# A transformer block with two expert layers around an attention: tokens routed in two sides, results stored in tile order and gathered by token on GpSimd, first attention pair inside the second expert pass

## The chip, the cores and the metric

The kernel runs on one core of one Trainium2 chip. The time is the device time of one execution, in microseconds (us), as the median of some runs. A profiled execution gives the rows shown below; their times count from the start of its span.

## The reference

4096 tokens of 128 channels (16 sequences of 256) pass an expert layer (FFN), an attention, and the same expert layer again. Each part adds to the residual:

```python
x = x + 0.5 * ffn(layernorm(x), Wg, bg, Wgu, bgu, Wd, bd)
x = x + attention(layernorm(x), W_attn, b_attn, W_proj, b_proj)   # 16 heads of 8 channels, causal
x = x + 0.5 * ffn(layernorm(x), Wg, bg, Wgu, bgu, Wd, bd)

def ffn(xt):                                # 16 experts, the best 2 of each token
    top_vals, top_idx = jax.lax.top_k(xt @ Wg.T + bg, 2)
    rw = softmax(top_vals)
    # of each chosen expert e: gate and up are the even and odd columns of xt @ Wgu[e] + bgu[e]
    gated = (clip(up, -7, 7) + 1.0) * (min(gate, 7) * sigmoid(1.702 * min(gate, 7)))
    out_e = gated @ Wd[e] + bd[e]           # the two are summed, weighted with rw
```

## The kernel before, in words

All engines run streams of their own, written by hand, with semaphores between them. Tokens lie in 32 tiles of 128; four tiles are a quad (`q`, 8 of them). `f` is 0 for the first expert layer and 1 for the second.

**Router.** Per quad, VectorE normalises the rows, TensorE transposes them and makes the logits, VectorE takes the best two and the rank of each token in its expert. GpSimd (POOL) then scatters the rows with indirect DMAs of 128 rows each into `rows_by_expert` in DRAM, 8 per quad, 64 in all. A row has 129 numbers: the last one is the number under which its result is to be stored (`K_NUM`); ScalarE copies each row for the second expert (`copy_rows`). In the second layer, the router of quads 0 to 5 (`MERGED`) runs inside the last turn of the attention.

**Table.** When all ranks are there, VectorE works out which expert and which rows each of 80 tiles has: 64 full ones' worth of rows, and 16 that pad each expert to a multiple of 128. SyncE (SP) copies the ends of the experts into `tab`, SP and ScalarE (ACT) zero 8 tiles each behind the last rows (`zero_tiles`), and SP copies the table into `tab`. `s_tab` counts these copies, and ScalarE and VectorE wait for it.

**Expert pass.** 80 tiles, two at a time (a pair `k`, four pairs a turn `t`, 40 pairs): SP loads the rows into `xt`, waiting for `s_goes` and `s_xTp` of the pair four before; TensorE transposes them (L1487), multiplies with gate and up (L1500) and down (L1512); ScalarE copies the weights (L717), evacuates the transposes and takes the sigmoid; VectorE gates (L1097 to L1100) and adds the down bias into `ysb` (L1128). It also makes the store targets (`going` L1106, `goes_to` L1124). GpSimd scatters each result tile by token number into `results_by_token` (L582), two per pair. `expert_pipeline` shifts the steps: in slot n, TensorE transposes pair n-1, does gate and up of pair n-2 and down of pair n-4.

**Attention.** When all results are stored, GpSimd loads them by quads with one plain DMA (`yg`); VectorE adds them weighted to `x_resident` (`combine`, L749), makes the statistics and normalises. TensorE transposes and projects q, k and v (L1155, L1161, L1168). q and k are split into three bf16 parts, which SP writes to DRAM several times over and reads back as `q_stack` and `k_stack`. The first scores need both stacks. Of 8 quads, quad x+2 is combined while quad x is in attention.

**Tail.** After the second expert pass the results are read with eight plain DMAs of SP and ScalarE, combined (L1140) and written out by quads.

## Time and the profile before

| | us |
|---|---|
| median of 3 runs | 784.53 (783.05 to 786.78) |
| the profiled execution's own time | 784.48 |
| its span | 782.8 |
| first scatters end, first expert pass begins (gate and up) | 103.7, 113.4 |
| first scores of the attention | 258.7 |
| second pass begins (gate and up) | 644.7 |
| last store issued, last combine ends | 752.9, 780.1 |

The span is what the engines' records cover; the time of the execution is 1.7 us longer. The stretches between the lines are: router, expert pass, first pair, attention with the second router, expert pass, tail.

### The profile page before, as it was taken

The page shows a single profiled execution, that of the slowest core. Times are in us where ns is not written, and L with a number is a line of the kernel's source. Part 1 is how long each engine was busy: PE and PEld are TensorE (multiplying, and loading weights), DVE is VectorE, ACT ScalarE, POOL GpSimd, SP SyncE. Part 2 cuts the span into 40 slices and gives each one's busy share as a digit, 9 for nine tenths or more (in the row PEclk, how much of TensorE's full clock was granted, in tenths as well). Part 3 has the DMA queues.
Part 4 walks back from the last instruction along what each step waited for, and adds up shares of the span by engine and source line. Part 5 has one row for each costly group of instructions (what it writes and reads, how often), then busy time and mean ns, then how long its engine had stood idle before and what let it go on. Part 6 is the DMA issues. An engine that isn't in the chain of part 4 may idle for free.

```text
span 782.8 us, 19236 instructions
## 1 busy us (share of the span) xinstructions
PE 514.2 (66%) x5867; PEld 328.6 (42%) x5867; DVE 512.6 (65%) x2750; ACT 300.9 (38%) x554; POOL 334.5 (43%) x348
## 2 busy tenths in 40 slices
PE   3368429888504579787978897978775319888600
PEld 2234117656302245454544454545452207655400
DVE  6865408777624577777777777879874507877618
ACT  1111028766201245353544454625342217766300
POOL 2777745777740010101010101020657744777740
PEclk9999999999855689897989798989896559999955
DMA  9411363333215170606060606050111163333237
GB/s 270 142 55 51 79 89 99 107 105 104 68 55 202 62 242 7 239 29 215 0 242 22 224 2 216 15 202 2 42 43 53 58 104 87 110 107 102 79 121 234
DMA packets 83468, 83.88 MB, mean 107 GB/s; under 512 B 10373, under 2 KB 74314, under 8 KB 83146
## 3 DMA queue, kind: packets, MB, share of 16 engines
q1 hardware_dynamic: 68618, 56.78, 24.4%
q0 software_dynamic: 10368, 23.15, 8.8%
q10 hardware_dynamic: 4416, 3.16, 1.8%
q8 instruction: 31, 0.51, 0.3%
q14 instruction: 35, 0.29, 0.1%
HBM read 43.03 MB, written 39.99 MB: 106 GB/s over the span
## 4 chain that ended last, share of the span: by engine, by line
DVE 23%; POOL 23%; PE 23%; issue 22%; DMA 4%; ACT 3%; DVEq 2%; SPq 1%; POOLq 0%; ACTq 0%
POOL results_by_token L582 12%; POOL rows_by_expert L549 10%; DVE by_token L799 5%; PE banks L1293 2%; DVE x_resident L1140 2%; PE banks L1243 2%; PE banks L1269 2%; DVE x_resident L749 2%; PE banks L1420 2%; PE banks L1218 2%; PE banks L1168 1%; PE banks L1161 1%; PE banks L1271 1%; PE banks L1234 1%; DVE upc L1098 1%
## 5 line engine op out<-in xcount | busy, mean ns | idle before, releaser
L582 POOL DMA_INDIRECT results_by_token<-ysb,goes_to x160 | 154.1, 963 | 73.8 <-issue 44.8
L799 DVE CUSTOM_DVE_ANT_0 by_token<-banks,konst_sb 128x128 f32<-128x128 f32 (+1 forms) x512 | 147.1, 352 | 38.3 <-issue 38.1
L616 ACT ACTIVATE pT<-banks 128x1536 f32<-128x1536 f32 x64 | 92.8, 1450 | 53.4 <-PE banks L1271 53.4
L717 ACT ACTIVATE pT<-w_experts 128x384 f32 x160 | 74.9, 516 | 69.7 <-DMA tab<-tabc 42.8
L1500 PE MATMUL banks<-xT,pT 128*64 128x128 f32 x1280 | 90.0, 284 | 10.4 <-DVE row_buf L1100 9.0
L549 POOL DMA_INDIRECT rows_by_expert<-by_token,posi x80 | 77.0, 963 | 28.5 <-issue 23.2
L1500 PEld LDWEIGHTS banks<-xT,pT 128*64 128x64 f32 x1280 | 70.7, 140 | 27.5 <-DVE row_buf L1100 16.5
L517 POOL CAST q_parts<-sig 128x512 bf16<-128x512 f32 x7 | 4.2, 604 | 152.4 <-DVE sig L787 152.4
L1487 PE MATMUL banks<-konst_sb,xt 128*128 128x128 f32 x160 | 35.6, 306 | 46.6 <-DMA xt<-rows_by_expert 45.9
L1512 PE MATMUL banks<-pT,row_buf 128*64 128x128 f32 x640 | 52.9, 285 | 15.5 <-DVE ysb L1128 13.1
L610 ACT ACTIVATE mT<-banks 128x256 bf16<-128x256 f32 x64 | 24.6, 384 | 92.3 <-PE banks L1218 92.3
L1293 PE MATMUL banks<-pT,by_token 128*32 128x256 f32 (+1 forms) x1024 | 59.6, 354 | 0.0
L1199 PE MATMUL banks<-k_stack,q_stack 64*128 64x256 bf16 x256 | 42.4, 288 | 22.1 <-DVE mraw L799 13.5
L1512 PEld LDWEIGHTS banks<-pT,row_buf 128*64 128x64 f32 x640 | 37.1, 139 | 27.7 <-issue 24.5
L1128 DVE TENSOR_TENSOR ysb<-banks,w_experts 128x128 f32<-128x128 f32 x160 | 39.2, 286 | 11.6 <-issue 0.2
L1243 PE MATMUL banks<-q_stack,k_stack 64*128 64x256 bf16 x256 | 44.5, 294 | 0.0
L1234 PE MATMUL banks<-mT,select 64*128 64x256 bf16 x256 | 44.0, 296 | 0.0
L729 ACT ACTIVATE sig<-banks 128x256 f32<-128x256 f32 x80 | 30.7, 384 | 34.3 <-PE banks L1500 28.9
L1293 PEld LDWEIGHTS banks<-pT,by_token 128*32 128x32 f32 x1024 | 28.1, 116 | 34.8 <-issue 25.0
L1218 PE MATMUL banks<-identb,mparts 128*64 128x128 bf16 x256 | 20.7, 245 | 33.6 <-DVE x_resident L820 20.3
L1097 DVE SCALAR_TENSOR_TENSOR sig<-banks,sig 128x256 f32<-128x256 f32 x80 | 33.8, 423 | 13.4 <-ACT sig L729 11.1
L1487 PEld LDWEIGHTS banks<-konst_sb,xt 128*128 128x128 f32 x160 | 16.6, 145 | 61.7 <-issue 58.1
(182 smaller groups left out, 1123.5 us busy)
## 6 DMA issues: line engine op xcount, KB each, us to landing
xt<-rows_by_expert SPq DMA_DIRECT2D x160, 64.5 KB
q_stack<-q_by_part SPq DMA_DIRECT2D x8, 1024.0 KB, 6.4
k_stack<-k_by_part SPq DMA_DIRECT2D x8, 1024.0 KB, 5.8
q_by_part<-q_parts SPq DMA_DIRECT2D x16, 384.0 KB, 3.1
k_by_part<-k_parts SPq DMA_DIRECT2D x16, 384.0 KB, 2.8
yg<-results_by_token POOLq DMA_DIRECT2D x8, 512.0 KB, 4.9
results_by_token<-ysb,goes_to POOLq DMA_INDIRECT x160
x_resident<-in_x SPq DMA_DIRECT2D x8, 256.0 KB, 5.5
```

Of the source, the lines that this page charges most:

```text
L549: pool.indirect_dma_start(out=rows_dram, out_offset=bass.IndirectOffsetOnAxis(ap=posi[:, c:c + 1], axis=0), in_=rows_of(f, q)[:, i, k, :], ...
L582: pool.indirect_dma_start(out=results_dram, out_offset=bass.IndirectOffsetOnAxis(ap=goes_to[:, 2 * k + i:2 * k + i + 1], axis=0), in_=ysb[ ...
L616: nc.scalar.activation(pT[:, s % 2, :], banks[:, 3:6, :].rearrange("p a q -> p (a q)"), ACT.Exp, scale=SCALE).then_inc(a_exp, 1)
L717: last = nc.scalar.activation(w_tile[:, 2 * k + i, :], w_all[:, bass.ds(experts[key][k % 2 * 2 + i], EW)], ACT.Identity)
L799: last = nc.vector.tensor_tensor_reduce(masked[:, (3 * g + qt) * P:(3 * g + 2 * qt + 1) * P], of, lag, 1.0, NEG * NEG_BELOW, ALU.add, ALU. ...
L1199: return nc.tensor.matmul(bank[1 + g % 2][:, c:c + T], q[r, pair, m, o + P:o + T], k[r, pair, m, o:o + T], start=g // 2 == 0, stop=g // 2 ...
L1234: nc.tensor.matmul(bank[3 + g % 2][:, g // 2 * T:(g // 2 + 1) * T], select[maxima(g), g, :], mT[maxima(g), s % 2, :], start=g // 2 == 0, s ...
L1243: nc.tensor.matmul(bank[3 + g % 2][:, c:c + T], k[r, pair, m, o:o + P], q[r, pair, m, o:o + T], start=False, stop=False)
L1293: last = nc.tensor.matmul(bank[6][g * QUARTER:(g + 1) * QUARTER, c + kt * P:c + T], of_head, w, start=j == 0 and kt == 0, stop=j == GRP - ...
L1487: last = nc.tensor.transpose(bank[k % 2][:, i * P:(i + 1) * P], xt[:, 2 * k + i, 0:C], ident)
L1500: last = nc.tensor.matmul(bank[2 + k % 2][h * HALF:(h + 1) * HALF, at:at + P], w_tile[:, 2 * k + i, which * F + h * HALF:which * F + (h + ...
L1512: last = nc.tensor.matmul(bank[6 + k % 2][h * HALF:(h + 1) * HALF, i * C:(i + 1) * C], gT[:, k, i * P + h * HALF:i * P + (h + 1) * HALF], ...
```

## The change

The tokens are routed in two sides of 16 tiles each, with counts, ranks and a table of their own. Each side has 32 tiles of rows and again 16 of padding, so 48 tiles (24 pairs, 6 turns) per pass, and there are now four passes `p` (0 and 1 in the first layer, 2 and 3 in the second), with 96 tiles per layer instead of 80. `expert_passes` runs the two passes of a layer without draining the pipeline in between.

```diff
-REGION = N + P
-TILES = N * TOPK // P + E
+SIDES = 2
+REGION = N // SIDES + P
+TILES = TSIDE * TOPK + E
```

SP does all zero tiles (16 a side) and, new, the stores of the results in tile order; it waits for them in its own order:

```diff
         def zero_tiles(eng, g):
-            with eng.Fori(0, E // 8) as e:
+            with eng.Fori(0, E // 4) as e:
...
+            def store(p, t, k):
+
+                sp.wait_ge(s_ysb[k], p * TURNS + (t + 1))
+                sp.dma_start(results_t[p % SIDES][:, bass.ds(t * DUOS + k, 1), :, :], ysb[:, k:k + 1, :, :]).then_inc(s_store[k], 16)
...
+                table_of(first)
+                sp.wait_ge(s_zero, 16 * (1 + E * (first + 1)))
+                sp.wait_ge(s_scat[0], 16 * TOPK * TSIDE * (f + 1))
+                load_turn(first, 0)
+                table_of(second)
+                experts(first)
+                sp.wait_ge(s_zero, 16 * (1 + E * (second + 1)))
+                sp.wait_ge(s_scat[1], 16 * TOPK * TSIDE * (f + 1))
+                load_turn(second, 0)
+                experts(second)
+                for k in range(1, DUOS):
+                    store(second, TURNS - 2, k)
+                for k in range(DUOS):
+                    if f == 0 and k == 1:
+                        stack_first(sp)
+                    store(second, TURNS - 1, k)
```

ScalarE and VectorE wait for both tables of a layer before its first pass:

```diff
+                def copy_weights(p, t, k):
+                    if p % SIDES == 0 and isinstance(t, int) and (t, k) == (0, 0):
+                        act.wait_ge(s_tab, 32 * (p + 2))
```

Rows have 128 numbers again, `copy_rows`, `going` and `goes_to` are gone. VectorE works out where each token's two results lie (`in_tiles`, 3 instructions a side), and GpSimd gathers them with one indirect DMA per 128 rows, 8 per quad: into `yg` for the attention, into `by_token` for the tail, side by side.

```diff
+            def gather(q, to, done):
+                for j in range(QUAD * TOPK):
+                    c = q * QUAD * TOPK + j
+                    pool.indirect_dma_start(
+                        out=to[:, j, :], out_offset=None,
+                        in_=results_dram[q // QSIDE], in_offset=bass.IndirectOffsetOnAxis(ap=tilepos[:, c:c + 1], axis=0)).then_inc(done, 16)
...
+                    for q in range(NQ):
+                        if q % QSIDE == 0:
+                            stored(SIDES + q // QSIDE)
+                        gather(q, last_results[:, q * QUAD * TOPK:(q + 1) * QUAD * TOPK, :], s_got[q])
```

The first attention pair is prepared by hooks in the last two turns of pass 1; on VectorE:

```diff
+                if (t, k) == (TURNS - 2, 0):
+                    combine(0)
+                if (t, k) == (TURNS - 2, 1):
+                    stats(0)
+                if (t, k) == (TURNS - 2, 2):
+                    normalise(0)
+                if (t, k) == (TURNS - 1, 1):
+                    parts_of_first(0)
+                if (t, k) == (TURNS - 1, 2):
+                    parts_of_first(1)
+                if (t, k) == (TURNS - 1, 3):
+                    combine(1)
+                if (t, k) == (TURNS, 0):
+                    stats(1)
+                if (t, k) == (TURNS, 1):
+                    normalise(1)
```

How the instructions stand now is shown at three places. On SP, in the loop of an expert pass, two pairs of one turn stood so before (L471 loads a tile of rows, L1592 reads row numbers from the table, ISA is address arithmetic):

```order
L1592 TENSOR_LOAD tab
L471 ISA
L471 DMA xt<-rows_by_expert 128x129
L471 ISA
L471 DMA xt<-rows_by_expert 128x129
L479 REGISTER_ALU
```

and one pair of the same loop stands so now (L459 loads, L464 stores two tiles at once):

```order
L459 ISA [waits s_xTp]
L459 DMA xt<-rows_by_expert 128x128
L459 ISA
L459 DMA xt<-rows_by_expert 128x128
L463 REGISTER_ALU
L464 ISA [waits s_ysb1]
L464 DMA results_by_tile<-ysb 128x2x128
```

Each pair has a third DMA on SP and a wait for VectorE's `ysb` between the loads of two pairs.

On SP, between the first loads of pass 2 and the loads behind them, the second table of the layer stands now (the loop L409 runs four times, four zero tiles each):

```order
L442 DMA tab<-zrow 1x16x1 [waits s_ends]
L409 UNCONDITIONAL_BRANCH [waits s_tab_ends]
L1644 TENSOR_LOAD tab
L411 DMA rows_by_expert<-zeros 128x128
L409 COMPARE_AND_BRANCH
L451 DMA tab<-tabc 1x48x1 [waits s_table]
L1644 TENSOR_LOAD tab [waits s_tab]
L459 ISA [waits s_xTp]
```

Before, there was one table of a layer, ahead of all loads, and its loop ran twice on SP and twice on ScalarE.

On VectorE, slot 16 of pass 1 (the gate of a pair, its `ysb`, then the hook) reads now:

```order
L1140 SCALAR_TENSOR_TENSOR sig<-banks,sig 128x256 [waits s_sig]
L1141 TENSOR_SCALAR upc<-banks 128x256
L1143 SCALAR_TENSOR_TENSOR gT<-upc,sig 128x256 [waits s_vec]
L1157 ISA [waits s_y,s_store0]
L1157 TENSOR_TENSOR ysb<-banks,w_experts 128x128
L755 SCALAR_TENSOR_TENSOR x_resident<-yg,wts,x_resident 128x128 [waits a_got]
L755 SCALAR_TENSOR_TENSOR x_resident<-yg,wts,x_resident 128x128 x3
```

The L755 instructions stood behind the whole pass before and now stand between two gates.

## Rows read from the trace of the kernel before

**Rows 1.** The page, chain that ended last: its costliest lines, share of the span.

```profile
POOL results_by_token L582 12%; POOL rows_by_expert L549 10%; DVE by_token L799 5%; PE banks L1293 2%; DVE x_resident L1140 2%; PE banks L1243 2%; PE banks L1269 2%; DVE x_resident L749 2%; PE banks L1420 2%; PE banks L1218 2%; PE banks L1168 1%; PE banks L1161 1%; PE banks L1271 1%; PE banks L1234 1%; DVE upc L1098 1%
```

**Rows 2.** The chain into the first pass: start us, length us, what.

```profile
103.70 4.93 DMA rows_by_expert<-by_token,posi
...
110.17 0.04 SPq L471
...
110.68 0.04 SPq L471
...
110.82 1.90 DMA xt<-rows_by_expert
```

**Rows 3.** GpSimd timeline, scatters: start us, us, what, idle before and its releaser.

```profile
64.57 0.96 POOL L549 DMA_INDIRECT rows_by_expert<-by_token,posi  x1 [0.31 <-issue]
65.83 0.95 POOL L549 DMA_INDIRECT rows_by_expert<-by_token,posi  x1 [0.30 <-issue]
```

**Rows 4.** TensorE timeline, first pass: its start, and down of two pairs.

```profile
113.44 1.98 PE L1500 MATMUL banks<-xT,pT 128*64 128x128 f32 x16
...
120.29 0.61 PE L1512 MATMUL banks<-pT,row_buf 128*64 128x128 f32 x8
...
122.12 0.61 PE L1512 MATMUL banks<-pT,row_buf 128*64 128x128 f32 x8
```

**Rows 5.** Two stretches: length, then PE, PEld, DVE, ACT, POOL busy, clock, DMA, GB/s.

```profile
229.00:253.00 24.00, 8.46 (x29) 4.10 (x29) 13.26 (x52) 2.57 (x4) 3.65 (x4) 0.50 0.43 145
440.00:480.00 40.00, 34.53 (x464) 20.03 (x456) 31.36 (x193) 20.19 (x26) 5.35 (x6) 0.91 0.42 137
```

**Rows 6.** VectorE timeline, one pair of the first pass and the next one's gate.

```profile
121.35 0.41 DVE L1097 SCALAR_TENSOR_TENSOR sig<-banks,sig 128x256 f32<-128x256 f32 x1
...
122.53 0.15 DVE L1124 COPY goes_to<-going 128x2 int32<-128x2 int32 x1
122.83 0.49 DVE L1128 TENSOR_TENSOR ysb<-banks,w_experts 128x128 f32<-128x128 f32 x2
...
123.30 0.42 DVE L1097 SCALAR_TENSOR_TENSOR sig<-banks,sig 128x256 f32<-128x256 f32 x1
```

**Rows 7.** SP timeline, first table: last four zero tiles, table copies.

```profile
97.08 1.88 SPq L414 DMA_DIRECT2D rows_by_expert<-zeros  x4
99.17 1.20 SPq L458 DMA_DIRECT2D tab<-tabc  x2
```

**Rows 8.** SP timeline, second table: the experts' ends, eight zero tiles.

```profile
622.08 0.59 SPq L446 DMA_DIRECT2D tab<-zrow  x1
624.45 5.05 SPq L414 DMA_DIRECT2D rows_by_expert<-zeros  x8
```

**Rows 9.** DMA issues, 88 to 111 us: count, KB each, median us to landing.

```profile
tab<-tabc SPq DMA_DIRECT2D x2, 0.3 KB, 7.6
```

**Rows 10.** VectorE timeline, first and last instruction of the first table.

```profile
90.93 0.21 DVE L1060 TENSOR_SCALAR zrow<-banks,konst_sb 16x1 int32<-16x1 f32 x1 [0.37 <-PE banks L1474]
...
93.83 0.17 DVE L1084 CAST tabc<-tabf 128x2 int32<-128x2 f32 x1
```

**Rows 11.** Timeline of all engines, last copy of the k parts, first scores.

```profile
247.01 0.46 SPq L400 DMA_DIRECT2D k_by_part<-k_parts  x1
...
258.68 0.39 PE L1199 MATMUL banks<-k_stack,q_stack 64*128 64x256 bf16 x1 [5.32 <-DMA k_stack<-k_by_part]
```

**Rows 12.** Timeline of all engines, the second pass begins.

```profile
639.05 0.94 ACT L717 ACTIVATE pT<-w_experts 128x384 f32 x2 [18.35 <-DMA tab<-tabc]
640.37 4.70 SPq L471 DMA_DIRECT2D xt<-rows_by_expert  x8
...
644.70 1.98 PE L1500 MATMUL banks<-xT,pT 128*64 128x128 f32 x16
```

**Rows 13.** The chain in the tail: start us, length us, what.

```profile
754.18 2.22 DMA results_by_token<-ysb,goes_to
...
776.69 2.20 DVE x_resident L1140 x8
```

More of the change, by code:

```diff
@@ new lines, in load_turn, with experts, stores_behind @@
+            def load_turn(p, t):
+                for k in range(DUOS):
+                    if k % 2 == 0:
+                        rows = registers(nc, sp, tab[0:1, p % SIDES, bass.ds(t * UNROLL + (TILES + 2 * k), 4)], SIDES * E * REGION)
+                    load(p, t, k, rows)
+                    stores_behind(p, t, k)
+            def experts(p):
+                load_turn(p, 1)
+                with sp.Fori(2, TURNS) as t:
+                    load_turn(p, t)
+            def stores_behind(p, t, k):
+                back = 2 if k < DUOS - 1 else 1
+                if not isinstance(t, int) or t >= back:
+                    store(p, t - back, (k + 1) % DUOS)
+                elif p % SIDES:
+                    store(p - 1, t - back + TURNS, (k + 1) % DUOS)
@@ L1132, in _, with later @@
+                def later(p, t, k):
+                    if (p, t) == (2, 0):
+                        if k == 0:
+                            in_tiles(2)
+                        if k == 2:
+                            in_tiles(3)
+                expert_passes(dve, f, (2, gate), (4, evac_y), chain=(ch, 2), hook=first_pair if f == 0 else later)
                 if f == 0:
@@ L1611, in slot, with turn @@
             turn, k2 = t + pair // DUOS, pair % DUOS
[L1612 removed]
+            if isinstance(turn, int) and turn >= TURNS:
                 continue
[L1614 to L1629 removed]
+            if isinstance(turn, int) and turn < 0:
+                if p % SIDES:
+                    step(p - 1, turn + TURNS, k2)
+                continue
+            step(p, turn, k2)
+        if hook and isinstance(t, int):
+            hook(p, t, k)
+    def turn(p, t):
+        for k in range(DUOS):
+            slot(p, t, k)
+    for p in range(f * SIDES, (f + 1) * SIDES):
+        peeled = 2 if p == 1 else 0
+        turn(p, 0)
+        turn(p, 1)
+        with eng.Fori(2, TURNS - peeled) as t:
+            if chain:
+                chain[0].begin(t - 2, chain[1] * DUOS)
+            turn(p, t)
+        if chain:
+            chain[0].end(TURNS - peeled - 2)
+        for t in range(TURNS - peeled, TURNS):
+            turn(p, t)
+    for k in range(DUOS):
+        slot(f * SIDES + 1, TURNS, k)
 _OUT = (B, T, C)
```

684 lines of the change are left out of this document (330 added, 354 removed).

## The prediction

> **What bounds the kernel now.** I read the page's chain first. Its two costliest lines are GpSimd's: the scatter of results, 12% of the span, and the scatter of rows, 10% [rows 1]. One scatter starts 1.26 us after the one before it (0.96 of work, 0.30 between) [rows 3]. A result tile costs one such scatter, so a pair of tiles costs 2.52 us, whatever the other engines do. Next comes what these could do. In the stretch before the four result buffers are full, TensorE issues down for two successive pairs 1.83 us apart [rows 4], and VectorE needs 1.95 us per pair, of which 0.30 is the copy of the targets and 0.07 what `going` adds [rows 6]: without both, about 1.58. So 40 pairs at 2.52 are GpSimd's time, and the pass is slower than its engines.
>
> Three stretches between passes are waits: the first pass starts only when all 64 row scatters have landed (the last one at 103.7 plus 4.9, then the loads; gate and up at 113.4) [rows 2, 4]; from the last result to the first scores at 258.7 one pair is prepared on a nearly idle core (TensorE 8.5 and VectorE 13.3 us busy in 24) [rows 5, 11]; the tail is one load and a chain of combines [rows 13].
>
> **Part by part.** I go through the kernel on the clock of the trace of before, and take two things for granted: the attention itself and the second router keep their length, and there I shift the clock.
>
> *First pass, start.* It needs only the 32 scatters of side 0, long done by then, but ScalarE's weight copies wait for both tables. VectorE's router is lengthened by the table of side 0, 3.1 us (90.9 to 94.0 [rows 10]), while GpSimd has a backlog of scatters and nobody else waits. So side 1's ends come at about 94.1. From there SP: 2.4 us to the first zero tile [rows 8]; then 16 tiles instead of 8. Four take 1.88 [rows 7]; two rounds take 5.05 [rows 8], so 1.29 lie between rounds, and four rounds are 11.4. Then 0.2 and two table copies in 1.2 [rows 7]. Their landing was 7.6 us from issue behind 16 zero tiles from two queues [rows 9]; one queue asks for half as much per us, and a small copy that finds the queues free lies within the 2.4 above [rows 8]. I take 3 from issue (bounds 2 and 7.6). Together 17.6 us, so both tables are there at 111.8 (110.8 to 116.4), weights 0.94 later plus 0.4 [rows 12], gate and up at 113.2. That is the start of before: nothing gained, the wait for scatters is replaced by one for SP.
>
> *Rate.* GpSimd is out of the loop, but SP gets a third DMA per pair. Two issues start 0.51 us apart [rows 2]. A turn of four pairs is now 12 of them, 6.1; the round's own cost (a register load and branch, 1.29 less the ordinary gap) about 0.9; a second register load 0.4; arithmetic and waits 0.3; and a store of 256 rows issues perhaps in 0.37 to 0.46 instead of 0.33 (the nearest is the copy of k parts, 0.46 [rows 11]), 0.3 per turn. That is 8.0 us per turn, **2.0 us per pair**: slower than TensorE's 1.83. Bounds: 1.83, if SP's instructions overlap or come cheaper, and 2.3, if every DMA of the turn takes the 0.46 (12 times 0.13 more). SP has four pairs of lead, so only its rate counts. Load 8 goes at about 119.4, load 47 at 39 × 2.0 later, 197.4; it is issued in 0.9 and lands in 1.9 [rows 2]: slot 48 at 200.2. Of the stores' traffic I count nothing: the 16 DMA engines are 43% busy at most in the stretches shown [rows 5].
>
> *First pair in pass 1.* VectorE's 13.3 us [rows 5], all but the last normalise (1.1), now lie in slots 40 to 48: 12.2, less 9 × 0.42 that it has free per slot, less some 2 that it may lag behind: 6.4. TensorE's part (8.5 at clock 0.50, so 4.2 at full) is covered by that. `ysb` of pair 44 is then ready at 209.1, and SP turns to the stacks: spreading q and k is six issues (2.8, at 0.46 each), and from the start of the last one to the scores it was 11.7 [rows 11], about 14.0 in all. **First scores at 223.1 instead of 258.7: 35.6 us saved.** Gather 1 starts behind the root of pair 0 (about 190.5) and lands at 203, when VectorE reaches it; if it is late, that comes on top. In the attention eight gathers per quad are 10.1 us of GpSimd in about 43 us, where it was busy 5.35 in 40 [rows 5]: they fit between the parts of one pair and the next.
>
> *Second pass, start.* Ends of side 0 at 622.1 [rows 8], its table at +17.6, 639.7; then eight loads (0.4 and 4.7 [rows 12]) to 644.8; and only then SP does side 1's table: another 17.6, 662.4. ScalarE waits for it, gate and up at 663.7 instead of 644.7 [rows 12]. **19.0 us lost.** What was hidden behind the scatters before is now in the open, twice, on one queue. The second `in_tiles` delays one gate in the filling pipeline, some 1 us, inside my rounding.
>
> *To the end.* Load 8 at 669.9 (half clock at the start), load 47 at 747.9, slot 48 at 750.7, last `ysb` 7.8 us later (four slots) at 758.5, stored by 761.2 (issue 0.5, landing 2.2 as the scatter's [rows 13]). Side 0's 32 gathers start when its stores have landed, near 717, and end near 758, just free. Side 1's begin at 761.2 and are all exposed: 32 × 1.26 = 40.4, 801.6, landing 1.3 after the last one's end. The trace has no gather; the nearest is the scatter of the same 128 rows of 512 bytes, so 1.26 it is (a gather at 0.96 back to back would save 9.6; with 0.3 more it costs 9.6). The last quad's combine (2.3) and the way out (2.7: before, from 780.1 to 782.8) give 807.9. The tail from the last result was 28.6 us (754.2 to 782.8) and is 49.4 now.
>
> **Sum.** 807.9 − 35.6 = 772.3, plus the 1.7 by which the profiled execution (784.48) exceeds its span: **774 us**. That execution is within 0.1 of the median of the runs shown, so I compare with 784.5: 10.5 faster, 1.3%.
>
> **A page against it.** Of SP the trace shows 0.51 us per issue, and that rate paces my passes. The Trainium skill ("DMA: Bandwidth & Descriptors", Issuing engines are not separate DMA queues) holds that starting DMAs on several engines saves only the time to initiate them, usually small beside the DMA itself. By the rows a load's issue is a fourth of its landing, and three a pair exceed TensorE's 1.83; by the page's view the move to SP would be nearly free, which is the first rival.
>
> **Rivals.**
> 1. *TensorE paces the passes.* For it: 1.83 was held for several pairs, and my 2.0 is built from parts, not seen. Against: the parts are all SP's own instructions, one behind the other. 39 × 0.17 twice is 13.3 less: 761. Chance 0.18.
> 2. *SP paces them still slower.* One mechanism: the store's 256 rows hold the queue, so that it and the loads behind it issue in 0.46 rather than 0.33. The trace has both: zero tiles in a row kept their pace, the copies of parts in a row did not. From 2.0 + 10.5/78 = 2.14 us per pair on the gain is gone; at 2.3 it is 78 × 0.3 = 23 more: 797, slower than before. About 0.17 for the part beyond 2.14, with 2.2 (790) its middle.
> 3. *GpSimd and VectorE block each other in the tail.* Combines now run beside gathers, both of them at SBUF. Before, scatters kept their 0.96 while VectorE worked on the router beside them [rows 3], which speaks against it; but no row has them beside combines. If each combine (2.2 per quad) stopped the gathers, side 1's four cost 9: 783, no change. Chance 0.08. The Trainium skill ("SBUF — State Buffer", Who interferes with whom) describes such a lock for VectorE operations with two SBUF inputs against a GpSimd operation that reads SBUF; no row here shows it.
> 4. *The tables come earlier or later than I think*, with landings at the ends of their bounds: 3 × 1 less, or 3 × 4.6 more (788). Chance 0.07, mostly no change.
>
> My forecast has 0.50 (766 to 780 by itself, from landings and VectorE's lag of ±2 each and a rate of ±0.05).
>
> **Numbers.** The range reaches to rival 1 below and to the middle of rival 2 above: 757 to 790. Below 757 and above 790 I leave 0.08 and 0.12. A measurement of this kernel tells 0.5%, some 4 us, from no change. Faster (below 780.6): my case nearly whole, rival 1, a little of the others, 0.69. Same: the edge of my case, rivals 3 and 4, 0.14. Slower: rival 2 and late tables, 0.17.
>
> **What the changed profile would show.** SP's loads 2.0 us apart per pair in the middle of a pass, with TensorE's transposes waiting for `xt`, and no gap between passes; gate and up of pass 0 at 113, of pass 2 some 40 us behind the last ends' copy (it was 22.6); first scores at 223; side 1's gathers back to back 1.26 apart for 40 us with TensorE silent. I am wrong if the loop on SP is not the pace, if the first gather is late for VectorE, or if the gathers in the attention push the parts of a pair behind its scores.

## The result: slower, where faster was forecast

| | before | after |
|---|---|---|
| median, us | 786.16 (783.05 to 787.12, 5 runs) | 791.99 (790.80 to 795.07, 5 runs) |
| ratio | | 1.0087, 95% interval [1.0055, 1.0119] |
| span of the profiled execution, us | 782.8 | 793.3 |

The change costs 0.9%. The forecast was 774 us; 792 lies outside its range, on the other side of no change.

How the stretches came out, on the clock of each profiled execution (the forecast's own points, and those of the rows below):

| stretch | before | forecast | after | after − forecast |
|---|---|---|---|---|
| to gate and up of the first pass | 113.4 | 113.2 | 110.7 | −2.5 |
| from there to the first scores | 145.2 | 109.9 | 128.4 | **+18.5** |
| to the copy of side 0's ends, second layer | 363.4 | 363.4 | 363.1 | −0.3 |
| to gate and up of the second pass | 22.6 | 41.6 | 38.3 | −3.3 |
| to the first exposed gather | | 97.5 | 104.8 | **+7.3** |
| to the end of the span | | 46.7 | 47.9 | +1.2 |

The last column adds up to 20.9, and 772.3 + 20.9 is the span, within rounding. The attention kept its length, and the two losses that were forecast (a later second pass, a tail of gathers) came in at nearly their size. What failed is the gain at the first pair, and the pace of the passes in both layers.

### The profile page after: what moved, and what is told of

Its sections match the earlier page's. It is cut to its first block, busy times and chain, and to the rows that moved or that the text cites. A ratio compares the mean times of both kernels' runs of the same rounds, so it can differ in the third digit from the quotient of the medians.

```text
span 793.3 us, 19957 instructions
## 1 busy us (share of the span) xinstructions
PE 531.3 (67%) x6287; PEld 353.9 (45%) x6287; DVE 525.7 (66%) x2691; ACT 317.9 (40%) x602; POOL 296.9 (37%) x308
## 4 chain that ended last, share of the span: by engine, by line
PE 29%; DVE 21%; SPq 18%; issue 16%; POOL 7%; DMA 3%; ACT 3%; DVEq 1%; ACTq 0%; POOLq 0%
SPq L459 8%; DVE by_token L805 5%; SPq L464 4%; POOL by_token L526 4%; POOL rows_by_expert L564 3%; PE banks L1469 3%; SPq L411 2%; PE banks L1327 2%; PE banks L1553 2%; PE banks L1517 2%; SPq L1644 2%; PE banks L1277 2%; PE banks L1303 2%; DVE x_resident L755 2%; PE banks L1461 2%
## 5 line engine op out<-in xcount | busy, mean ns | idle before, releaser
L564 POOL DMA_INDIRECT rows_by_expert<-by_token,posi x120 | 115.7, 964 | 57.2 <-issue 35.0
L1553 PE MATMUL banks<-xT,pT 128*64 128x128 f32 x1536 | 109.3, 286 | 31.3 <-ACT pT L731 17.0
L731 ACT ACTIVATE pT<-w_experts 128x384 f32 x192 | 90.0, 516 | 77.4 <-DMA tab<-tabc 61.7
L1553 PEld LDWEIGHTS banks<-xT,pT 128*64 128x64 f32 x1536 | 85.6, 141 | 48.5 <-ACT pT L731 31.8
L526 POOL DMA_INDIRECT by_token<-results_by_tile,tilepos x64 | 61.4, 959 | 105.5 <-DMA results_by_tile<-ysb 86.6
L526 POOL DMA_INDIRECT yg<-results_by_tile,tilepos x64 | 61.6, 963 | 81.1 <-DMA results_by_tile<-ysb 62.7
L1140 DVE SCALAR_TENSOR_TENSOR sig<-banks,sig 128x256 f32<-128x256 f32 x96 | 40.6, 423 | 62.2 <-ACT sig L741 60.7
L1564 PE MATMUL banks<-pT,gT 128*64 128x128 f32 x768 | 59.5, 276 | 4.4 <-DVE ysb L1157 4.4
L1157 DVE TENSOR_TENSOR ysb<-banks,w_experts 128x128 f32<-128x128 f32 x192 | 46.7, 283 | 15.6 <-issue 12.7
L1564 PEld LDWEIGHTS banks<-pT,gT 128*64 128x64 f32 x768 | 45.9, 139 | 5.4 <-DVE gT L1143 5.1
L1461 PE MATMUL banks<-konst_sb,by_token 128*128 128x128 f32 x60 | 14.4, 384 | 46.3 <-DVE by_token L932 38.3
L1541 PEld LDWEIGHTS banks<-konst_sb,xt 128*128 128x128 f32 x192 | 20.4, 146 | 54.5 <-issue 43.6
```

Of the source, the lines that this page charges most:

```text
L526: pool.indirect_dma_start(out=to[:, j, :], out_offset=None, in_=results_dram[q // QSIDE], in_offset=bass.IndirectOffsetOnAxis(ap=tilepos[: ...
L564: pool.indirect_dma_start(out=rows_dram, out_offset=bass.IndirectOffsetOnAxis(ap=posi[:, c:c + 1], axis=0), in_=rows_of(f, q)[:, i, :], in ...
L731: last = nc.scalar.activation(w_tile[:, 2 * k + i, :], w_all[:, bass.ds(held[key][k % 2 * 2 + i], EW)], ACT.Identity)
L1157: last = nc.vector.tensor_tensor(ysb[:, k, i, :], bank[6 + k % 2][:, i * C:(i + 1) * C], w_all[:, bass.ds(held[key][k % 2 * 2 + i] + EW, C ...
L1541: last = nc.tensor.transpose(bank[k % 2][:, i * P:(i + 1) * P], xt[:, 2 * k + i, :], ident)
L1553: last = nc.tensor.matmul(bank[2 + k % 2][h * HALF:(h + 1) * HALF, at:at + P], w_tile[:, 2 * k + i, which * F + h * HALF:which * F + (h + ...
```

## The profile after

The page's chain, by engine and by line, share of the span:

```profile
PE 29%; DVE 21%; SPq 18%; issue 16%; POOL 7%; DMA 3%; ACT 3%; DVEq 1%; ACTq 0%; POOLq 0%
SPq L459 8%; DVE by_token L805 5%; SPq L464 4%; POOL by_token L526 4%; POOL rows_by_expert L564 3%; PE banks L1469 3%; SPq L411 2%; PE banks L1327 2%; PE banks L1553 2%; PE banks L1517 2%; SPq L1644 2%; PE banks L1277 2%; PE banks L1303 2%; DVE x_resident L755 2%; PE banks L1461 2%
```

Where GpSimd's scatters stood [rows 1], SP's queue stands now: loads L459, stores L464, zero tiles L411, table loads L1644. The scatter of results is gone, the 32 exposed gathers are L526.

SP's timeline in the middle of pass 0 (start us, length us, what):

```profile
138.06 0.85 SPq L459 DMA_DIRECT2D xt<-rows_by_expert  x2
139.20 0.41 SPq L464 DMA_DIRECT2D results_by_tile<-ysb  x1
...
146.25 0.85 SPq L459 DMA_DIRECT2D xt<-rows_by_expert  x2
```

Two loads and a store per pair, and the next turn begins 8.19 us after this one: 2.05 us per pair, where I had worked out 2.0. But the loop has rows of another kind in it. The same timeline 20 us later, and the DMA queues of that moment (queue, packets, MB, share of the 16 engines):

```profile
157.43 2.17 SPq L459 DMA_DIRECT2D xt<-rows_by_expert  x2
```

```profile
q1 hardware_dynamic: 571, 0.27, 34.6%
q8 instruction: 1, 0.02, 3.4%
```

Two loads take 2.17 us instead of 0.85, and a 16 KB block of instructions is fetched in just these 3 us (157.6 to 159.2 by its packet). Over the whole trace 12 of SP's 288 loads and stores take more than 0.6 us, 10.9 us in excess of the ordinary 0.34, and 10 of the 12 lie over such a fetch. In all, load 47 of pass 1 goes 82.7 us behind load 8 (2.12 per pair), and the forecast had 78.0.

SP's timeline at the start of pass 0, and its longest wait there:

```profile
109.14 7.69 SPq L459 DMA_DIRECT2D xt<-rows_by_expert  x8
119.80 0.41 SPq L464 DMA_DIRECT2D results_by_tile<-ysb  x1
120.97 0.86 SPq L459 DMA_DIRECT2D xt<-rows_by_expert  x2
```

```profile
SPq L464 <- DVE ysb L1157: 3.0, 1, 3.0
```

Load 8 stands behind the store of pair 0 on SP, and SP waits 3.0 us for that pair's `ysb`. So load 8 goes 10.3 us behind the first gate and up, where the forecast had 6.2; in pass 2 it goes 9.7 behind.

VectorE's timeline over three hooks (L755 combine, L773 statistics, L785 normalise; the gate is L1140):

```profile
192.40 2.31 DVE L755 SCALAR_TENSOR_TENSOR x_resident<-yg,wts,x_resident 128x128 f32<-128x128 f32 x8
194.62 0.41 DVE L1140 SCALAR_TENSOR_TENSOR sig<-banks,sig 128x256 f32<-128x256 f32 x1
...
199.32 1.11 DVE L785 TENSOR_SCALAR xnT<-x_resident,a_mv,a_rs 128x128 f32<-128x128 f32 x4
200.34 0.41 DVE L1140 SCALAR_TENSOR_TENSOR sig<-banks,sig 128x256 f32<-128x256 f32 x1
...
203.20 0.42 DVE L1140 SCALAR_TENSOR_TENSOR sig<-banks,sig 128x256 f32<-128x256 f32 x1 [1.25 <-ACT sig L741]
...
207.27 0.42 DVE L1140 SCALAR_TENSOR_TENSOR sig<-banks,sig 128x256 f32<-128x256 f32 x1 [2.16 <-ACT sig L741]
```

and TensorE's in the same slots:

```profile
200.57 0.63 PE L1189 MATMUL banks<-konst_sb,xnT 128*128 128x128 f32 x4 [2.15 <-DVE xnT L785]
...
220.03 0.66 PE L1564 MATMUL banks<-pT,gT 128*64 128x128 f32 x8 [2.86 <-DVE ysb L1157]
223.98 1.09 PE L1189 MATMUL banks<-konst_sb,xnT 128*128 128x128 f32 x4 [3.29 <-DVE xnT L785]
```

Gates come 2.8 to 4.1 us apart. First VectorE is full and TensorE waits for it, for 5.4 us of it in hooks of its own (the transposes of L1189 need `xnT`). Then it is the other way round: VectorE is idle 1.25 and 2.16 for a sigmoid whose matmuls are late. Part of that is the granted clock, which fell from 1.00 to 0.50 for 3.4 us at 202.0. Two stretches of 2 us show it (columns as in [rows 5]), first of this kernel and then of a second execution of it on another chip, `e2_control` below:

```profile
202.00:204.00 2.00, 2.00 (x18) 1.67 (x14) 0.77 (x3) 0.77 (x3) 1.48 (x2) 0.50 0.65 175
202.00:204.00 2.00, 2.00 (x24) 1.41 (x24) 1.37 (x5) 1.70 (x4) 1.53 (x2) 1.00 0.75 203
```

In that stretch 16 matmuls of gate and up take 1.40 us and not 1.09, and the two of L1195 2.05 and not 1.13; gate and up of pair 43 comes 4.4 us behind that of pair 42, in the control 2.7.

SP's timeline behind the hooks, and the first scores:

```profile
220.33 1.02 SPq L389 DMA_DIRECT2D q_by_part<-q_parts  x2
...
223.92 0.96 SPq L394 DMA_DIRECT2D k_by_part<-k_parts  x1
225.27 0.70 SPq L397 DMA_DIRECT2D q_stack<-q_by_part  x1
230.09 0.37 SPq L397 DMA_DIRECT2D k_stack<-k_by_part  x1
```

```profile
239.08 0.39 PE L1233 MATMUL banks<-k_stack,q_stack 64*128 64x256 bf16 x1 [12.96 <-DMA k_stack<-k_by_part]
```

From the start of the last copy into `k_by_part` (the spreading of the parts) to the scores it is 15.2 us, where it was 11.7 [rows 11].

The second layer's tables on SP, and the pass behind them:

```profile
602.19 0.57 SPq L442 DMA_DIRECT2D tab<-zrow  x1
604.95 11.06 SPq L411 DMA_DIRECT2D rows_by_expert<-zeros  x16
616.23 1.18 SPq L451 DMA_DIRECT2D tab<-tabc  x2
619.23 4.33 SPq L459 DMA_DIRECT2D xt<-rows_by_expert  x8
623.62 0.52 SPq L442 DMA_DIRECT2D tab<-zrow  x1
625.93 10.31 SPq L411 DMA_DIRECT2D rows_by_expert<-zeros  x16
636.45 1.16 SPq L451 DMA_DIRECT2D tab<-tabc  x2
```

```profile
640.53 1.76 PE L1553 MATMUL banks<-xT,pT 128*64 128x128 f32 x14 [17.02 <-ACT pT L731]
```

This is the serial chain of the forecast, step by step: 16 zero tiles in 11.06 and 10.31 (forecast 11.4), twice, with TensorE idle. In the tail GpSimd's gathers run back to back, 1.25 us apart, beside VectorE's combines:

```profile
745.36 0.94 POOL L526 DMA_INDIRECT by_token<-results_by_tile,tilepos  x1 [3.25 <-DMA results_by_tile<-ysb]
746.61 0.94 POOL L526 DMA_INDIRECT by_token<-results_by_tile,tilepos  x1 [0.30 <-issue]
...
784.16 0.95 POOL L526 DMA_INDIRECT by_token<-results_by_tile,tilepos  x1 [0.30 <-issue]
786.70 2.32 DVE L1177 SCALAR_TENSOR_TENSOR x_resident<-by_token,wts,x_resident 128x128 f32<-128x128 f32 x8 [7.66 <-DMA by_token<-results_by_tile,tilepos]
```

## The experiments

The runs were made on several chips. On two of them (the runs e1 and e3) the kernel before took 927 us instead of some 785, so these runs are compared only with each other, stretch by stretch (none of them is the changed kernel unedited); the runs e2 and e4 are on chips that take 788 and 783 us for it.

### On the chip that takes 927 us

**One store for two pairs**, `e1_store_two` (SP: 10 DMAs per turn instead of 12; VectorE and GpSimd wait for the stores that are left):

```diff
             def store(p, t, k):
-
-                sp.wait_ge(s_ysb[k], p * TURNS + (t + 1))
-                sp.dma_start(results_t[p % SIDES][:, bass.ds(t * DUOS + k, 1), :, :], ysb[:, k:k + 1, :, :]).then_inc(s_store[k], 16)
+                if k % 2 == 0:
+                    return
+                sp.wait_ge(s_ysb[k], p * TURNS + (t + 1))
+                sp.dma_start(results_t[p % SIDES][:, bass.ds(t * DUOS + k - 1, 2), :, :], ysb[:, k - 1:k + 1, :, :]).then_inc(s_store[k], 16)
```

> The changed kernel with one edit: SP stores two pairs (four tiles) with one DMA instead of one pair, so a turn of an expert pass has 10 DMAs on SP and not 12. Theory A (SP's DMA issues pace the passes at 2.05 us per pair): two issues of 0.51 us less per turn give 1.8 us per pair, where TensorE's 1.83 takes over; some 78 pairs x 0.2 = 16 us less, about 776 us against 792. Rival B (the pace is set elsewhere, by transfers or by the long issues of 1 to 2 us that come every 10 us or so in SP's loop): less than 4 us, about 790.

**Zero tiles on two engines**, `e1_split_zero`:

```diff
-        def zero_tiles(eng, g):
-            with eng.Fori(0, E // 4) as e:
+        def zero_tiles(eng, g, half):
+            with eng.Fori(0, E // 8) as e:
...
+                for p in (2 * f, 2 * f + 1):
+                    act.wait_ge(s_tab_ends, 16 * (p + 1))
+                    zero_tiles(act, p % SIDES, 1)
```

> The changed kernel with one edit: of each side's 16 zero tiles ScalarE issues 8 and SP 8, two rounds of four on each, as before the change there were for a layer. Theory A (SP's serial tables are the wait ahead of both layers' passes): two rounds are 5.05 us and four were 11.4, so each table is 6.3 us shorter; pass 2 has two in the open, pass 0 one: gate and up of pass 2 at 628 and not 640.5, of pass 0 at 105 and not 110.7, 19 us less in all, 773. Rival B (zero tiles from two queues make the table's copies land later, 7.6 us as in the kernel before and not 3): half of that is given back, 783.

**The first pair behind the pass**, `e1_late_pair`:

```diff
         if hook and isinstance(t, int):
-            hook(p, t, k)
+            if p != 1:
+                hook(p, t, k)
...
-        peeled = 2 if p == 1 else 0
+        peeled = 0
...
+    if hook and f == 0:
+        for t in range(TURNS - 2, TURNS + 1):
+            for k in range(DUOS):
+                hook(1, t, k)
```

> The changed kernel with the first attention pair prepared behind pass 1 instead of in its last two turns (the hooks of all engines are called after the last slot, SP starts the stacks behind all stores). Theory A (the hooks made slots 40 to 48 of pass 1 some 10 us longer, so they hid only part of their work): first scores at 246 and not 239.1, 7 us more, 799. Rival B (all of the 15 us of VectorE's and TensorE's work was hidden): 15 us more or beyond, 807.

**A tail of plain loads**, `e1_plain_tail`:

```diff
-                        gather(q, last_results[:, q * QUAD * TOPK:(q + 1) * QUAD * TOPK, :], s_got[q])
+                        at = q % QSIDE * QUAD * TOPK * P
+                        pool.dma_start(last_results[:, q * QUAD * TOPK:(q + 1) * QUAD * TOPK, :],
+                                       results_dram[q // QSIDE][at:at + QUAD * TOPK * P, :].rearrange("(n p) c -> p n c", p=P)).then_inc(s_got[q], 16)
```

> The changed kernel, but in the tail GpSimd loads each quad's 1024 result rows with one plain DMA in tile order instead of eight gathers by token (the order by token is left out, so the results are combined with the wrong tokens). Theory A (side 1's 32 gathers, 38.8 us back to back behind the last store, are all exposed): the tail from the last store's landing falls from 48.8 to about 22 us, 27 us less, 765. Rival B (the loads of 512 bytes per row and the combines bound the tail as well): 15 us less, 777.

Measured, where the kernel before took 926.8: 935.8 (store_two), 945.3 (split_zero), 946.9 (late_pair), 884.2 (plain_tail). Four readings hold within this chip:

- *Zero tiles.* In the second layer it is 39.1 us from the start of VectorE's first table to gate and up with the tiles split, and 48.4 in late_pair, whose tables are the unedited ones. SP's timeline of split_zero, second table:

```profile
733.39 0.52 SPq L442 DMA_DIRECT2D tab<-zrow  x1
735.75 4.94 SPq L411 DMA_DIRECT2D rows_by_expert<-zeros  x8
740.91 1.16 SPq L451 DMA_DIRECT2D tab<-tabc  x2
743.73 1.93 SPq L459 DMA_DIRECT2D xt<-rows_by_expert  x4
```

  4.94 against 10.31, and the copies land no later (2.8 us from issue to the next load either way): theory A for the zero tiles, 9.3 of the 12.6 us that it gives for pass 2, and rival B's late copies are not there. Theory A's gain ahead of pass 0 did not come: gate and up is at 134.2 there, and at 131.1 to 131.7 in the other three, because VectorE made side 1's ends 6.7 us later (115.5 for 108.8 in late_pair).
- *The tail.* From the last down matmul to the end it is 21.5 us with plain loads and 51.9 and 51.8 in split_zero and late_pair; in the changed kernel on its first chip it was 51.8. So the gathers cost 30 us there, theory A.
- *The first pair* came to its scores no later than with the hooks (136 us behind the first gate and up, 139 and 141 in split_zero and plain_tail). Neither theory allowed for that.
- *The stores* brought the scores 10 us nearer to the first gate and up (130).

### The same edits beside the changed kernel

> The changed kernel itself, once more: the chip of the last four runs took 927 us for the kernel before, where 786 had been measured, so differences there say little against runs elsewhere. Both theories: the ratio to the kernel before is 1.009 on a chip that takes 785 us for it; if this chip too is slow, all comparisons of this call are made with this run.

> One store on SP for two pairs, as in e1_store_two, now beside a run of the changed kernel. Theory A (SP's issues pace the passes): 16 us less than the changed kernel, of which 8 are there at the first scores. Rival B (pace set elsewhere): less than 4 us.

> The first attention pair prepared behind pass 1, as in e1_late_pair, now beside a run of the changed kernel. Theory A (the hooks hide part of their work): first scores some 7 us later than in the changed kernel, counted from the first gate and up. Rival B (all of the 15 us were hidden): 15 us later. Rival C (the hooks cost the pass as much as they hide; on the slow chip the scores came no later than without them): within 3 us.

**The tables rearranged**, `e2_tables`:

```diff
                     if isinstance(t, int) and (t, k) == (0, 0):
-                        act.wait_ge(s_tab, 32 * (p + 2))
+                        act.wait_ge(s_tab[p % SIDES], 32 * (f + 1))
...
-                table_of(first)
+                table_of(sp, first)
...
                 load_turn(first, 0)
-                table_of(second)
                 experts(first)
...
                     for q in range(MERGED - 1, NQ):
                         scatter(q)
+                    table_of(pool, 3)
...
                     positions(MERGED - 1)
+                    table(2)
```

(the same on VectorE, and `table_of(pool, 1)` behind the scatters of the first layer.)

> The changed kernel with the tables rearranged: GpSimd copies the ends, zeroes the tiles and copies the table of side 1 behind its last scatter of each layer, SP does side 0's alone; ScalarE and VectorE wait only for the table of the pass that they begin; VectorE makes side 0's table of the second layer in the middle of the router of the last two quads and not behind it. Theory A (the gaps ahead of passes 0 and 2 are SP's serial tables and nothing else): gate and up of pass 0 at 98 and not 110.7, of pass 2 some 5 us behind VectorE's last table instead of 22, at 606 and not 640.5; 46 us less in all, ratio to the kernel before 0.95. Rival B (what is behind them is also late: the row scatters of side 1, or GpSimd's 19 DMAs at 1 us each beside the pass): half of it is given back, ratio 0.98.

| | median us | ratio to before, interval | gate/up 0 | first scores | VectorE's ends of side 0 | gate/up 2 | last down | end |
|---|---|---|---|---|---|---|---|---|
| e2_control | 791.9 | 1.0043 [1.0025, 1.0062] | 110.4 | 237.9 | 601.4 | 640.0 | 740.3 | 792.3 |
| e2_store_two | 770.1 | 0.9757 [0.9722, 0.9792] | 110.6 | 227.4 | 589.3 | 627.6 | 718.7 | 770.9 |
| e2_late_pair | 793.1 | 1.0074 [1.0049, 1.0100] | 110.4 | 238.3 | 596.5 | 635.0 | 734.1 | 786.0 |
| e2_tables | 744.9 | 0.9452 [0.9410, 0.9495] | 97.7 | 222.8 | 567.3 | 590.2 | 690.2 | 744.4 |

*Stores.* 22 us, more than theory A's 16: 10.7 from gate and up to the first scores, 9.2 in passes 2 and 3. The same 70 us of passes 0 and 1 in both kernels (length, then PE, PEld, DVE, ACT, POOL busy with their instructions, clock, DMA share, GB/s), the changed kernel first:

```profile
120.00:190.00 70.00, 63.71 (x902) 51.46 (x902) 55.71 (x174) 55.31 (x139) 7.60 (x8) 1.00 0.47 132
```

```profile
120.00:190.00 70.00, 67.89 (x970) 55.26 (x966) 60.17 (x198) 59.11 (x149) 7.61 (x8) 1.00 0.53 144
```

A pair is 26 matmuls, so 902 are 34.7 pairs, 2.02 us each, and 970 are 37.3, 1.88 each. In the waits of the first window TensorE stands 6.2 us for `xt` (12 times, 1.9 the longest); in the second it is 0.7 us, once, and SP has fallen from 18% of the chain to 6%:

```profile
PE 43%; DVE 22%; issue 13%; POOL 9%; SPq 6%; ACT 3%; DMA 3%; DVEq 1%; ACTq 0%; POOLq 0%
```

In store_two 9 issues are still long, 8 of them over a 16 KB fetch, for 8.6 us in excess, and in this window TensorE hardly waits for a load. The pace itself gives what theory A said: gate and up comes 6.9 us earlier at pair 40, ahead of the first hook, and 9.1 at the last pair of passes 2 and 3 (0.19 per pair), 16.0 together. The rest of the gain is a side effect of the edit. Without a store of its own, pair 44 no longer stands ahead of the stacks, so SP begins the spreading 0.5 us behind `ysb` of pair 43 (99.8 us behind gate and up, and 107.2 in the control), 4.0 before `ysb` of pair 44 is there; and from the spreading to the scores it is 17.0 and not 20.4. The hooked slots give 4.0 of the 6.9 back; the clock fell in them (6.8 us at 0.50).

*The pair behind the pass.* Rival C: 127.8 us from gate and up to the first scores, and 127.5 with the hooks. SP's timeline without them:

```profile
222.78 0.90 SPq L389 DMA_DIRECT2D q_by_part<-q_parts  x2
...
226.26 1.19 SPq L394 DMA_DIRECT2D k_by_part<-k_parts  x1
...
232.57 0.37 SPq L397 DMA_DIRECT2D k_stack<-k_by_part  x1
```

In the control the spreading starts at 217.54, 5.2 us earlier, but the scores come 20.4 us behind it and not 15.5. The pass itself is 14.0 us longer with the hooks (last down at 222.9 and not 208.9, from the same start). At `ysb` of pair 44, behind which SP turns to the stacks, it is 10.3 us later (106.7 and 96.4 behind gate and up), and some 0.7 of that was there before the first hook. Neither of the two executions has the fall of the clock in these slots. (The profiled execution of late_pair ended 5 us below its median; that lies behind the first scores, where it took 358 us to the ends of side 0 and the others 362 to 364.) The DMA queues from the first spreading to the scores (queue, packets, MB, share of the 16 engines), in the control and then in late_pair:

```profile
q1 hardware_dynamic: 4645, 4.71, 72.3%
q0 software_dynamic: 256, 0.52, 12.1%
```

```profile
q1 hardware_dynamic: 3584, 4.19, 84.4%
q0 software_dynamic: 160, 0.33, 9.8%
```

The DMA engines are over 0.8 busy in this stretch. With the hooks the last stores of the pass and a whole gather are in it (eight DMAs; late_pair has five such there), 5.23 MB in 20.4 us for 4.52 in 15.5. At the rate of late_pair (0.29 MB per us) the 0.71 MB more are 2.4 of the 4.9 us. But the bytes alone don't set the length: store_two moves 5.42 MB in this stretch of its own, in 17.0 us. What goes with the length is when GpSimd's gather for the third pair starts. It starts 2.3 us behind the first spreading in the two profiles of the changed kernel, in e2_tables and in three of the runs on the chips that take 927 us, and there the stretch takes 18.1 to 20.4. It starts 6.7 to 9.5 behind it in the other runs with hooks, and there the stretch takes 15.9 to 17.9. In late_pair one gather is over 2 us behind the first spreading and the next begins 11.3 behind it, with 15.5. No run moved that gather alone.

*Tables.* Theory A, 47 us: pass 0 begins at 97.7, behind the router and no longer behind SP, and pass 2 at 590.2, 4.5 us behind the start of VectorE's last table (585.65):

```profile
97.65 1.76 PE L1555 MATMUL banks<-xT,pT 128*64 128x128 f32 x14
```

```profile
569.81 10.39 SPq L411 DMA_DIRECT2D rows_by_expert<-zeros  x16
...
583.97 9.88 SPq L458 DMA_DIRECT2D xt<-rows_by_expert  x14
```

Side 0's zero tiles lie beside the router now. (Its ends come 19 us earlier here because VectorE makes that table earlier, so that column does not compare.) Of the 47.9 us of span, 12.7 lie ahead of pass 0, 2.4 up to the first scores, 34.7 from there to gate and up of pass 2; the tail is 2.1 longer. The three parts of the edit were not run one by one. Side 1's row scatters run until 603 us, beside pass 2, and cost nothing that the span shows: the pass takes 100.0 us from gate and up to the last down, the control's 100.3.

### Together

> The changed kernel with two edits together, the rearranged tables (alone 745 us where the changed kernel took 792) and one store for two pairs (alone 770). Theory A (the waits for the tables and SP's pace are separate, each in its own stretch): the gains add, 47 + 22 = 69 us, 723. Rival B (with the tables early, the passes or the first gather wait for something else, such as side 1's scatters): at most half of the 22 remains, 734 or more.

**Pair 1 behind the last slot**, `e3_pair1_late` (combine, stats and normalise of pair 1 on VectorE in hook (TURNS, 3), TensorE's transposes with them):

```diff
-                if (t, k) == (TURNS - 1, 3):
-                    combine(1)
-                if (t, k) == (TURNS, 0):
-                    stats(1)
-                if (t, k) == (TURNS, 1):
-                    normalise(1)
+                if (t, k) == (TURNS, 3):
+                    combine(1)
+                    stats(1)
+                    normalise(1)
```

> The changed kernel, with pair 0 prepared in the last two turns of pass 1 as it is, but pair 1 (combine, statistics, normalise on VectorE, its transposes on TensorE, their evacuation) behind the last slot, where the engines wait for the stacks. Theory A (in these slots VectorE and TensorE are both fully used, so every hook makes the pass longer by its whole time; those of pair 1 are 4.8 us on VectorE and a wait of TensorE of some 3): first scores 6 us earlier than in the changed kernel, 786. Rival B (the DMA traffic of the stacks, at 0.73 to 0.78 of all engines, bounds the scores whatever the slots do): less than 2 us.

> The tail with one plain DMA per quad in tile order (the order by token is left out, so the results are combined with the wrong tokens), as in e1_plain_tail, now on a chip with the usual times if this is one. Theory A (side 1's 32 gathers are exposed and nothing else is): 30 us less than the changed kernel, 762, all of it behind the last store. Rival B (side 0's gathers beside pass 3 slowed that pass as well): passes 2 and 3 are shorter too, by 3 us or more.

> Rearranged tables, one store for two pairs, and pair 1 behind the last slot. Theory A: 723 less the 6 us of e3_pair1_late, 717. Rival B (pair 1 is hidden already once the passes run at TensorE's pace): 723.

These four met a chip with 926.9 us for the kernel before: 903.8 (both), 956.2 (pair1_late), 896.5 (plain_tail), 899.3 (best). The tail is 21.5 us with plain loads again (e1: 21.5). All but plain_tail have passes 2 and 3 some 34 to 40 us longer than its 107, while side 0's gathers run (below, under the hardware). Three of them were run once more on another chip:

> The kernel of e3_both again, on a chip that takes some 786 us for the kernel before, if one is given. Theory A (the gains of the tables and of the stores add): 723, ratio 0.92. Rival B (one of them hides the other): 734 or more.

> The kernel of e3_pair1_late again. Theory A (hooks make the pass longer by their whole time, since TensorE has no slack to catch up with): scores 6 us earlier than in the changed kernel, counted from the first gate and up (122 and not 127.5 us behind it). Rival B (the stacks' traffic bounds the scores): 126 or more.

> The kernel of e3_best again. Theory A: 6 us less than e4_both, 717. Rival B: as e4_both, 723.

| | median us | ratio to before, interval | gate/up 0 | first scores | gate/up 2 | last down | end |
|---|---|---|---|---|---|---|---|
| e4_both | 726.1 | 0.9286 [0.9263, 0.9308] | 97.2 | 212.1 | 577.6 | 668.9 | 723.1 |
| e4_pair1_late | 789.0 | 1.0061 [1.0032, 1.0089] | 110.3 | 233.6 | 635.9 | 736.7 | 788.9 |
| e4_best | 724.8 | 0.9247 [0.9219, 0.9275] | 97.3 | 212.6 | 579.9 | 671.7 | 726.6 |

The gains of tables and stores add: from the control's span of 792.3, 47.9 and 21.4 off give 723.0, and the span is 723.1. By the ratios, against kernels before on different chips, the gain is some 9 us less than the sum.

Moving pair 1 brings the first scores nearer to the first gate and up: 123.3 us, for 127.5 in the control and 128.4 in the first execution of the changed kernel. The second of these is the like one, since the clock fell for 3.4 us in the hooked slots of both (at 200.7 and 202.0) and not in the control's. Against it the gain is 5.1 us, near theory A's 6: 2.5 up to the start of the spreading (107.1 for 109.6) and 2.6 from there to the scores (16.2 for 18.75). Against the control it is 4.2, all of it behind the start of the spreading. So the slots became shorter by some 2.5, which the control's luckier clock hides. The 2.6 go with the third pair's gather, which waits for pair 1's statistics: it starts 7.7 us behind the spreading in pair1_late, and 2.3 in the changed kernel. In time the move shows nothing: 1.0061 against 1.0043 and 1.0087 for the changed kernel, and 0.9247 against 0.9286 in the fast one, with intervals that overlap. So theory A's 786 and 717 did not come. The version that beats both kernels is `e4_both`: rearranged tables and one store for two pairs, 7.1% under the kernel before.

## Why the prediction was wrong

Three terms of the sum were too small, and one of them had its mechanism wrong. In the changed kernel's own profile, the +18.5 before the first scores divide so:

| | forecast | after | more |
|---|---|---|---|
| gate and up of pair 0 to load 8 | 6.2 | 10.3 | 4.1 |
| load 8 to load 47 | 78.0 | 82.7 | 4.7 |
| load 47 to the start of the spreading | 11.7 | 16.7 | 5.0 |
| start of the spreading to the first scores | 14.0 | 18.75 | 4.7 |

**Rate** is the largest: 8.8 us here and 8.1 in passes 2 and 3 (3.5 up to load 8, 4.6 behind it), nearly 17 of the 20.9 us. That SP is the pace was right, and store_two shows it: with two issues less per turn the pairs come 16.0 us earlier in the two layers. The size was wrong in two places. "SP has four pairs of lead, so only its rate counts" left out that load 8 stands behind the store of pair 0, and so behind its `ysb`: SP waits 3.0 and 2.4 us for it. And a pair takes 2.05 in an ordinary turn and 2.12 on the average, since the long issues (10.9 us over the whole trace) were in no term. Without hooks too, gate and up of pair 46 comes 93.0 us behind the first, and the forecast had 87.0. A little of the 4.7 belongs to the hooks: in late_pair load 47 is 80.6 behind load 8.

**First pair in pass 1** had the mechanism wrong: "TensorE's part … is covered by that" and VectorE's 12.2 us "less 9 × 0.42 that it has free per slot, less some 2 that it may lag behind: 6.4". At `ysb` of pair 44, the point that the forecast means, the hooks cost 10.3 us between control and late_pair, and 9.6 of it behind the first hook: 3 to 4 more than 6.4. In the first execution of the changed kernel it is 2.5 more again, 1.6 of that where the clock fell. At the last down it is 14.0. The idle 0.42 was real in the rows, but it could not be spent: TensorE stands 5.4 us for `xnT` and 2.9 for `ysb` in these slots, and once behind it has only 2.0 − 1.83 per slot to catch up. That the two banks of gate and up tie the engines together is read from the code and not tested; how the 10.3 divide between VectorE's hooks, TensorE's hooks and the waits was not measured. The outcome is plain: first scores 127.5 us behind gate and up with the hooks, 127.8 without.

**The stacks** were forecast as "about 14.0 in all" and take 18.75 from the first spreading. The last spreading starts 3.6 us behind the first and not 2.3, and from there it is 15.2 us and not 11.7. No run shows 14.0: the shortest is late_pair's 15.5, without stores beside it. The forecast had nothing beside the stacks. Some 2 to 3 us of the excess go with the gather that GpSimd starts 2.3 behind the first spreading (above); where it starts later, the stretch still takes 15.5 to 17.0, and up to 17.9 on the chips that take 927 us. Why the gather costs so much stays open.

Rival 2 named the direction (SP slower than 2.0) with another mechanism, the store's 256 rows holding the queue. The rows refute that: a load behind a store keeps its 0.33, the store takes 0.41. Rival 1 is false: 2 of 12 issues per turn less shorten the passes by 16.0 us. By the Trainium skill ("DMA: Bandwidth & Descriptors", Issuing engines are not separate DMA queues) the time to initiate DMAs is usually small beside the DMA; this loop is not the usual case. The Trainium skill ("Perfetto Trace Analysis", DMA Optimizations) says that balancing the DMAs over sync, scalar and GpSimd may help where descriptor generation, and not the transfer, is the bottleneck; no run did that with the loads and stores.

**Second pass, start** was right: 38.3 for 41.6, and rearranging the tables alone takes back what they cost and more: 34.7 us between the first scores and gate and up of pass 2. Rival 4's late landings did not come; the tables were 3 us early. **To the end** was right for the tail (47.9 for 46.7): 1.25 per gather for 1.26, and 30 us dearer than plain loads on the chips that take 927 us, the only ones on which the plain tail ran. Rival 3 is false: the gathers keep their 0.94 beside the combines, so the lock that the Trainium skill describes ("SBUF — State Buffer", Who interferes with whom) does not show here.

The balance of the change is then: the first scores come 19.6 us earlier than before (none of it from the hooks: without them they come at 238.3 and not 237.9), the second start costs 15.7, and passes 2 and 3 with the tail cost 14.6 more (152.7 us for 138.1).

## What to carry to other kernels

Work that is hooked into a pipelined loop should be priced near its full length when the engines are close to the pace: here 12.2 us of VectorE's work cost 10.3 and saved nothing. Idle shares of coupled engines are not a budget. When an engine's work moves to a queue, count that queue's issues per turn against the next slowest engine, look at what stands ahead of each load in it, and leave it a reserve: at 2.05 against 1.83 it had none. And look which tables, waits and zero fills stand ahead of a pass in one queue: waiting for just what the pass reads, on an engine that is free, was worth 47 us where the change had cost 6.

## What was not expected of the hardware

- A DMA issue on SP that meets the fetch of a 16 KB block of instructions often takes 0.7 to 2.2 us instead of 0.33: of the issues over 0.6 us, 10 of 12 lie over a fetch in this trace, 9 of 10 in the control, 8 of 9 in store_two. Some 13 such fetches fall into the four passes. The Trainium skill ("Runtime: NRT & Kernel Launch", Instruction fetch mechanics) has the 16 KiB blocks and calls the cost of crossing from one to the next mostly hidden; by these rows it is not hidden from SP's issues. That the fetch is the cause rests on this coincidence; no run took a fetch away.
- TensorE's granted clock differs between executions of like kernels in the hooked slots. It fell from 1.00 to 0.50 some 82 to 91 us behind the first gate and up, for 3.4 us in the changed kernel, `e4_both` and `e4_pair1_late` and for 6.8 in `e2_store_two` and `e4_best`, and not at all there in `e2_control` and `e2_tables`. TensorE had stood idle 2.15 us for `xnT` shortly before it fell in the changed kernel, and 2.44 in the control, where it did not fall. What decides it stays open; in the changed kernel it was worth 1.6 us.
- On both chips that take 927 us for the kernel before, TensorE crawls in pass 3 beside side 0's gathers. In `e1_split_zero` gate and up of one pair comes 39 us behind that of the pair before, with single matmuls 1.4 to 2.8 us apart and once 13.3 (columns as above), at half clock from 811 us on:

```profile
780.00:800.00 20.00, 17.47 (x250) 13.97 (x246) 15.21 (x48) 15.28 (x39) 0.00 (x0) 1.00 0.47 132
805.00:840.00 35.00, 11.04 (x74) 6.66 (x70) 3.79 (x12) 2.67 (x7) 26.52 (x28) 0.58 0.29 77
```

  The gathers keep their pace (28 in 35 us) and TensorE's waits name almost nothing but issue. Without the gathers (plain_tail, both times) passes 2 and 3 take 102 and 107 us, with them 133 to 139 in the e1 runs and 141 to 147 in the e3 runs; in the control, on another chip, the passes with the same gathers take 100 us, and late_pair's passes 0 and 1 without any take 98.5. These chips lose time elsewhere too, where no gather runs: the first gate and up of late_pair comes at 131.7 for 110.4, and from the first scores to the copy of the ends it is 439 us for 358. What differs between the chips stays open.
